# Second self attention of a two-block transformer kernel: the row maximum is seeded into PSUM by ScalarE, and the value products go in groups of two slots

## What is computed

```python
h = layer_norm(hidden_states, norm1_g, norm1_b)
q = (q_in @ wq).reshape(b, n, H, HD).transpose(0, 2, 1, 3)     # H, HD = 16, 64
k = (kv_in @ wk).reshape(b, l, H, HD).transpose(0, 2, 1, 3)
v = (kv_in @ wv).reshape(b, l, H, HD).transpose(0, 2, 1, 3)
scores = jnp.einsum('bhnd,bhld->bhnl', q, k) * scale
probs = jax.nn.softmax(scores, axis=-1)
out = jnp.einsum('bhnl,bhld->bhnd', probs, v)
hidden_states = out.transpose(0, 2, 1, 3).reshape(b, n, H * HD) @ wo + bo + hidden_states
```

## Time and profile before

| | us |
|---|---|
| runs | 4218.38, 4223.74, 4226.12 |
| median | 4223.74 |
| span of the profiled execution | 4217.9 |
| second self attention in it, first pair to the end of its last work | about 1912 to 3434 |

### The profile page before, as it was taken

One profiled execution on the slowest core, in us unless ns is written; L12 is line 12 of the kernel. 1 busy time (PEld: TensorE's weight loads), 2 busy tenths in 40 slices (PEclk: granted clock), 3 DMA queues, 4 the chain that ended last, 5 costly groups with the idle time before them and its releaser, 6 DMA issues. The chain is left out here.

```text
span 4217.9 us, 64445 instructions
## 1 busy us (share of the span) xinstructions
PE 3909.5 (93%) x24639; PEld 2598.3 (62%) x24639; DVE 2770.9 (66%) x4547; ACT 1839.2 (44%) x2746; POOL 1859.2 (44%) x1203
## 2 busy tenths in 40 slices
PE   3799999994998997998999999999999979999899
PEld 2533443433557886884666666666666647777787
DVE  6599999953536654435676767676766737665665
ACT  1267777771443333442333333333333334444333
POOL 1288970001203002005777777877787753222200
PEclk9789999996779998997999999999999989999899
DMA  4734434405622005883211111121112010000100
GB/s 159 180 56 77 59 57 48 42 2 94 102 43 52 22 13 197 306 308 103 75 51 51 64 63 51 51 76 51 51 51 76 26 31 10 10 10 1 42 15 17
DMA packets 314421, 294.96 MB, mean 70 GB/s; under 512 B 133420, under 2 KB 237292, under 8 KB 313860
## 3 DMA queue, kind: packets, MB, share of 16 engines
q1 hardware_dynamic: 311460, 281.88, 25.7%
q0 software_dynamic: 2656, 8.97, 0.7%
HBM read 161.92 MB, written 127.28 MB: 69 GB/s over the span
## 5 line engine op out<-in xcount | busy, mean ns | idle before, releaser
L1741 POOL TENSOR_TENSOR f_sums<-f_sums,f_probs 128x1024 f32<-128x1024 f32 x384 | 915.5, 2384 | 154.8 <-ACT f_probs L1860 117.1
L1860 ACT ACTIVATE f_probs<-f_st 128x1024 f32<-128x1024 f32 x512 | 525.0, 1027 | 938.7 <-PE f_st L1906 933.9
L1758 DVE TENSOR_REDUCE f_mx<-f_s 128x1 f32<-128x512 f32 x1024 | 659.8, 686 | 380.7 <-PE f_s L1883 369.4
L1369 DVE TENSOR_REDUCE f_mx<-f_s 128x1 f32<-128x512 f32 x1024 | 638.6, 683 | 50.8 <-PE f_s L1501 28.4
L1481 ACT ACTIVATE f_probs<-f_st 128x512 f32<-128x512 f32 x1024 | 535.9, 601 | 225.6 <-PE f_st L1518 225.5
L1883 PE MATMUL f_s<-f_k,f_q 64*128 64x512 f32 x3072 | 515.0, 415 | 18.6 <-DMA f_k<-k 12.5
L1906 PE MATMUL f_st<-f_q,f_k 64*128 64x512 f32 x3072 | 485.2, 390 | 1.1 <-ACT f_probs L1860 1.0
L1920 PE MATMUL f_acc<-f_probs,f_v 128*64 128x512 f32 x2048 | 465.0, 596 | 0.0
L1883 PEld LDWEIGHTS f_s<-f_k,f_q 64*128 64x128 f32 x3072 | 341.2, 189 | 166.6 <-issue 112.1
L1906 PEld LDWEIGHTS f_st<-f_q,f_k 64*128 64x128 f32 x3072 | 366.4, 184 | 25.9 <-ACT f_probs L1860 3.8
L1518 PE MATMUL f_st<-f_q,f_k 50*128 50x512 f32 x1024 | 332.7, 472 | 6.9 <-ACT f_probs L1481 6.8
(11 more groups left out here) (320 smaller groups left out, 7874.5 us busy)
## 6 DMA issues: line engine op xcount, KB each, us to landing
q<-f_stage SPq DMA_DIRECT2D x80, 512.0 KB, 2.9
k<-f_stage SPq DMA_DIRECT2D x80, 512.0 KB, 2.9
f_q<-q SPq DMA_DIRECT2D x32, 1024.0 KB, 5.0
f_k<-k SPq DMA_DIRECT2D x32, 1024.0 KB, 7.3
v<-f_v_stage SPq DMA_DIRECT2D x64, 256.0 KB, 3.1
f_v<-v SPq DMA_DIRECT2D x32, 512.0 KB, 8.5
f_q<-q SPq DMA_DIRECT2D x96, 128.0 KB, 4.2
f_k<-k SPq DMA_DIRECT2D x96, 128.0 KB, 6.9
```

Source lines behind the costliest of these rows:

```text
L1369: v.tensor_reduce(mx[:, i % 2, c:c + 1], bank[u % 4][:, :], AX_X, ALU.max).then_inc(s_free, 1)
L1741: g_.tensor_tensor(out, out, probs[:, n % NP, :, :], ALU.add).then_inc(sum_done, 1)
L1758: v.tensor_reduce(mx[:, i % 2, c:c + 1], bank[u % 3][:, :], AX_X, ALU.max).then_inc(s_free, 1)
L1860: a_.activation(probs[:, s % NP, :, :], stb[s % 2][:, :, :], ACT.Exp, scale=L.scale).then_inc(p_ready, 1)
```

## The change

- The rows of maxima no longer go through TensorE. VectorE copies the turned maxima once, a DMA writes them to DRAM (`self.shift`), a second DMA reads them back to all 128 partitions (`shift`), and ScalarE copies a 128x1024 part of them into the PSUM buffer before shifted runs (`seed`). shifted is then six matmuls that accumulate onto it. `prime` runs once at the start of the stage, four matmuls that write the buffers with start=True.
- ScalarE's order becomes exp of slot n, seed of slot n + 2, exp of slot n + 1, seed of slot n + 3. The seed waits for the exp of the same buffer.
- values go in groups of two slots (GROUP = 2), two blocks of two slots behind their exp (LAG = 2).
- The order of a block of two slots on TensorE is pair, shifted, shifted, pair, and then project, weigh and values where they are due. EARLY is 8 instead of 3. turn comes at the start of block 4, weigh in blocks 0 and 4, project in blocks 3 and 7 (of the half whose normalise is in block 1 or 5).
- high sits behind the exp of slots 4 and 12 (5 and 13 before), low behind the adds of slots 5 and 13 (6 and 14 before).
- q and k of step i + 2 are loaded when shifted of step i - 1 is through, v when its values are.

```diff
-        NP, DEPTH, GROUP, EARLY, RING0 = 8, 3, 4, 3, 3
+        NP, DEPTH, GROUP, EARLY, RING0 = 8, 3, 2, 8, 3
+        BLOCKS, PER_HALF, LAG = SLOTS // GROUP, KC // GROUP, 2
...
+        def y_at(i, b):
+            if b == BLOCKS - 1:
+                return i, 0
+            return (i - 1, 1) if b == PER_HALF - 1 and i > 0 else None
...
+                    sp.dma_start(self.shift[par].rearrange("(c t) -> c t", t=P), mm[par][:, :]).then_inc(m_out[par], 16)
+                    sp.wait_ge(m_out[par], 16 * (i // 2 + 1))
...
+                    sp.dma_start(shift[par][:, :, :].rearrange("p h t -> p (h t)"), self.shift[par].partition_broadcast(P))\
+                        .then_inc(m_in[par], 16)
...
-                            if n == 6 and i > 0:
+                            if n == 5 and i > 0:
                                 low(2 * i - 1)
-                            if n == 14:
+                            if n == 13:
                                 low(2 * i)
...
-                    v.tensor_scalar(mm[par][:, 0, :].bitcast(U32), rows.bitcast(U32), HI12, None,
-                                    ALU.bitwise_and).then_inc(m_cut, 1)
-                    dve.wait_ge(m_cut, i + 1)
-                    v.tensor_tensor(mm[par][:, 1, :], rows, mm[par][:, 0, :], ALU.subtract).then_inc(m_split, 1)
-                    dve.wait_ge(m_split, i + 1)
-                    dve.sem_inc(s_free, 1)
+                    v.tensor_copy(mm[par][:, :], rows).then_inc(s_free, 1)
...
+                def seed(n):
+                    i, s = n // SLOTS, n % SLOTS
+                    half = s // KC
+                    if n >= 2:
+                        act.wait_ge(p_ready, n - 1)
+                    if s == 0:
+                        act.wait_ge(m_in[i % 2], 16 * (i // 2 + 1))
+                    a_.activation(stb[s % 2][:, :, :], shift[i % 2][:, :, half * HALF:(half + 1) * HALF], ACT.Copy).then_inc(seeded, 1)
...
-                        if s == 5 and i > 0:
+                        if n + 2 < STEPS * SLOTS:
+                            seed(n + 2)
+                        if s == 4 and i > 0:
                             high(2 * i - 1)
-                        if s == 13:
+                        if s == 12:
                             high(2 * i)
...
-                    for r, (kk, qq) in enumerate(((0, 0), (0, 1), (1, 0), (None, None))):
+                    for r, (kk, qq) in enumerate(((0, 0), (0, 1), (1, 0))):
...
+                    for b in range(BLOCKS):
+                        if turn_at(i, b):
+                            turn(i + 1)
+                        first, last = next_pair(i, GROUP * b), next_pair(i, GROUP * b + 1)
+                        if first:
+                            pair(*first)
+                        shifted(i, GROUP * b)
+                        shifted(i, GROUP * b + 1)
+                        if last:
+                            pair(*last)
+                        if y_at(i, b):
+                            k, half = y_at(i, b)
+                            project(2 * k + half)
+                        if den_at(i, b):
+                            weigh(*den_at(i, b))
+                        if values_at(i, b):
+                            values(*values_at(i, b))
```

More of the change, by code:

```diff
@@ L1638, in attend_wide @@
             vs = [sb(f"v{k}", [P, KC, 2, W]) for k in slots_of]
-            m = [sb(f"m{k}", [P, N], F32R) for k in two]
-            mones = sb("mones", [P, P], F32R)
+            shift = [sb(f"shift{k}", [P, 2, N]) for k in two]
             ones = sb("ones", [P, W])
@@ L1645, in attend_wide @@
             negm = sb("negm", [P, 2 * QB])
-            mm = [sb(f"mm{k}", [2 * QB, 2, P]) for k in two]
+            mm = [sb(f"mm{k}", [2 * QB, P]) for k in two]
             on = sb("on", [P, 2, HALF])
@@ L1850, in high @@
                     a_.activation(o_hi[:, half, :], on[:, half, :], ACT.Copy).then_inc(hi_done, 1)
+                act.wait_ge(primed, 1)
+                seed(0)
+                seed(1)
                 for i in range(STEPS):
@@ L1893, in turn, with prime @@
                     t.transpose(bank[u % 3][0:2 * QB, 0:P], negm[:, :], ident[:, :]).then_inc(s_ready, 1)
+                def prime():
+                    pe.wait_ge(q_in[0], 32)
+                    for k in two:
+                        for h in range(2):
+                            ins = t.matmul(stb[k][:, h, :], k_[0][:, 0, 0:P], q[0][:, 0, 0:HALF], start=True, stop=True)
+                    ins.then_inc(primed, 1)
                 def shifted(i, s):
-                    cur, par, half, c = i % DEPTH, i % 2, s // KC, s % KC
-                    if s == 0:
-                        pe.wait_ge(m_in[par], (i // 2 + 1) * 64)
-                    pe.wait_ge(p_ready, i * SLOTS + s + 1)
+                    cur, half, c = i % DEPTH, s // KC, s % KC
+                    pe.wait_ge(seeded, i * SLOTS + s + 1)
                     cols, keys = slice(half * HALF, (half + 1) * HALF), slice(c * P, (c + 1) * P)
-                    for r, (kk, qq) in enumerate(((0, 0), (0, 1), (1, 0), (None, None))):
+                    for r, (kk, qq) in enumerate(((0, 0), (0, 1), (1, 0))):
                         for h in range(2):
                             rows = slice(64 * h, 64 * h + 64)
-                            lhs = mones[rows, :] if kk is None else k_[cur][rows, kk, keys]
-                            rhs = m[par][rows, cols] if kk is None else q[cur][rows, qq, cols]
-                            ins = t.matmul(stb[s % 2][:, h, :], lhs, rhs, start=r == 0, stop=r == 3, tile_position=(64 * h, 0))
+                            ins = t.matmul(stb[s % 2][:, h, :], k_[cur][rows, kk, keys], q[cur][rows, qq, cols], start=False, stop=r == 2,
+                                           tile_position=(64 * h, 0), skip_group_check=True)
                     ins.then_inc(st_ready, 1)
@@ L1912, in values @@
                         pe.wait_ge(v_in[cur], (i // DEPTH + 1) * 16)
[L1913 to L1915 removed]
+                    pe.wait_ge(p_ready, i * SLOTS + GROUP * grp + GROUP)
+                    half = 2 * i + grp // PER_HALF
+                    if grp % PER_HALF == 0 and half > 0:
+                        pe.wait_ge(on_done, half)
                     for j in range(GROUP):
@@ L1946, in project @@
                         ins.then_inc(s_ready, 1)
+                prime()
                 for j in range(2 * QB):
@@ L1953, in _ @@
                 for i in range(STEPS):
-                    for s in range(SLOTS):
-                        shifted(i, s)
-                        if s == 3 and i > 0:
-                            weigh(i - 1, 1)
-                            values(i - 1, 3)
-                        if s == 7:
-                            if i > 0:
-                                project(2 * i - 2)
-                            values(i, 0)
-                        if s == 11:
-                            weigh(i, 0)
-                            values(i, 1)
-                        if s == 15:
-                            if i + 1 < STEPS:
-                                turn(i + 1)
-                            if i > 0:
-                                project(2 * i - 1)
-                            values(i, 2)
-                        if s < SLOTS - EARLY:
-                            if i + 1 < STEPS:
-                                pair(i + 1, EARLY + s)
-                        elif i + 2 < STEPS:
-                            pair(i + 2, s - SLOTS + EARLY)
+                    for b in range(BLOCKS):
+                        if turn_at(i, b):
+                            turn(i + 1)
[6 more added lines that the diff above has]
+                            pair(*last)
+                        if y_at(i, b):
+                            k, half = y_at(i, b)
+                            project(2 * k + half)
+                        if den_at(i, b):
+                            weigh(*den_at(i, b))
+                        if values_at(i, b):
+                            values(*values_at(i, b))
                 weigh(STEPS - 1, 1)
-                values(STEPS - 1, 3)
-                project(2 * STEPS - 2)
+                for b in range(LAG):
+                    values(*values_at(STEPS, b))
                 project(2 * STEPS - 1)
```

120 lines of the change are left out of this document (58 added, 62 removed).

## The result

The changed kernel (called **after** from here on, and the kernel before **before**) takes 4258.41 us (median of 4 runs, 4256.39 to 4282.32), the kernel before beside it 4224.57 (4 runs, 4218.38 to 4226.12). The ratio is 1.0098, 95% interval 1.007 to 1.0125: 0.98% slower, 34 us. The forecast was 4282, +58; the measured +34 lies inside its outer bounds, 4228 to 4312, and under the +40 to +75 to which it gave 60%.

A forecast was written before the change was run, and what follows sets the result against it. TensorE, full at 46.5 us a step, was the bound: -2.0 own time, +2.5 and +0.9 waits make 47.9, +45 over some 31 steps; ends +13 give +58, 4282 us. Range +40 to +75 (60%), outer bounds 4228 to 4312.

The forecast's parts named there:

- the reciprocal: Pair's second bank behind VectorE's reciprocal after weigh: TensorE waits 0.46 us, twice a step, +0.9 us a step.
- low was late: Project in blocks 3 and 7 waits for GpSimd's low: 1.2 us each, +2.5 us a step.
- the price of a change of shape: TensorE switching between row-halved and column-halved matmuls: 0.41 us per new group of values, +1.6 us a step.

## What to carry to other kernels

A matmul that goes is worth its time from start to start only if nothing else comes due in it; lay out the chains that it covered, engine by engine and from the same origin, and put the producer one place earlier before the cover is taken away. A wait should be costed with the others in place and without them: the reciprocal was worth 0.48 us while low was late and 0.87 after. And the price of a change of shape has to be read behind the instruction that will stand there, since the gap to the next start also holds the rest of what ran before it, and with it how far apart two heads ran.

## What the runs showed of the hardware

- A copy of 128x1024 on ScalarE takes 1029 ns from SBUF to PSUM and exp the other way 1016; an exp and a seed in turn take 2.00 us in the run of the seeds in the old order, 0.04 less than the two durations: the seed starts 0.03 after the exp's end, and the next exp 0.07 before the seed's (exp at 2609.93 for 1.01, seed at 2610.97 for 1.03, exp at 2611.93).
- ScalarE can write values that aren't zero into a bank of PSUM, and matmuls then accumulate on them: 512 seeds do it here, behind one round of matmuls with start=True into the same banks at the start of the stage. No run leaves that round out, so its part is not shown.
- The way of 8 KB from VectorE's SBUF tile to DRAM and back to 128 partitions (1 MB written) takes 6.3 to 7.0 us, from turn's matmul (with VectorE's copy) to the first seed, where the one broadcast in the earlier trace rows had 11.0 to landing.
- The granted clock of a stretch in which TensorE waits in turn with VectorE was 0.50 in one execution and 1.00 in another, without a difference in that part of the program: 2.01 or 1.52 us for a pair. In after it fell to 2.01 for two pairs and rose again, within one execution (1949.52, 1951.53, 1953.55, then 1.52 apart; granted clock 0.50 from 1947 to 1953).
- With three banks, VectorE's two reductions of 1.29 us and a hand-over of 0.23 let a pair start each 1.52 us at best, in the prologue of after and in the old order with turn behind slot 8 alike.
- Two heads' matmuls on the two halves of the rows run together or 0.12 apart, by the order around them (the two `f_m` matmuls of 512 columns last 0.40 or 0.51); the entry into the column-halved shape takes 0.08 or 0.20 with it.
